# Four chained graph layers on one core: the attended rows written inside the last loop, and edge rows gathered onto a shift

## The reference, cut to what matters

```python
x = _layernorm(x + _L0_gnn_ref(...))        # edge messages, two dense products, norm
x = _layernorm(x + _L1_gnn_ref(...))        # (out - mean) * rsqrt(var) * gamma + beta, leaky relu, + x
x = _layernorm(x + _L2_gnn_ref(...))        # equivariant messages over edges
x = _layernorm(x + _L3_gnn_ref(...))        # attention over edges

# inside layer 3, over the edges that share a src:
aw = jnp.einsum('ehf,ehf->eh', q[src], k[dst])
m = jax.ops.segment_max(aw, src); e = jnp.exp(aw - m[src])
denom = jax.ops.segment_sum(e, src)
out = jax.ops.segment_sum((e / denom[src])[:, :, None] * v[dst], src)
```

## Time and profile before

| | |
|---|---|
| time of 3 runs, median (lowest to highest) | 2148.97 us (2148.57 to 2158.34) |
| the profiled execution | 2156.94 us, its span 2155.2 us |
| busy share of the span | PE 84%, DVE 67%, ACT 53%, POOL 44% |
| mean granted TensorE clock | 0.896 of full speed |
| DMA | 350.61 MB, mean 163 GB/s |

### The profile page before, as it was taken

How to read it: one execution, slowest core, us unless ns; L and a number is a source line. 1 busy time by engine, 2 the same in 40 slices (tenths; PEclk the granted TensorE clock), 3 DMA queues, 4 the chain that set the end, 5 groups by cost and what they waited for, 6 DMA issues and landing times. The chain is left out here.

```text
span 2155.2 us, 24520 instructions
## 1 busy us (share of the span) xinstructions
PE 1803.9 (84%) x5525; PEld 933.2 (43%) x5525; DVE 1434.7 (67%) x2621; ACT 1149.2 (53%) x2356; POOL 949.1 (44%) x1070
## 2 busy tenths in 40 slices
PE   5999999599999999999999995961881588998840
PEld 2444444244444444444444443531771344544420
DVE  5365554177777777777777773517995578787876
ACT  1344434255555555555555552224883878877853
POOL 2212102166666666656666663544553232333236
PEclk8999999799999999999999997985555689999965
DMA  7752102534444454444444445554556887878774
GB/s 250 250 206 63 27 13 31 142 134 172 171 159 166 157 172 172 165 164 155 169 172 172 163 153 188 105 87 156 110 119 178 257 242 221 238 212 241 200 212 144
DMA packets 167421, 350.61 MB, mean 163 GB/s; under 512 B 30481, under 2 KB 30962, under 8 KB 166838
## 3 DMA queue, kind: packets, MB, share of 16 engines
q1 hardware_dynamic: 130838, 247.28, 32.4%
q0 software_dynamic: 33168, 98.01, 20.4%
q10 hardware_dynamic: 3344, 4.51, 0.7%
HBM read 177.32 MB, written 153.71 MB: 154 GB/s over the span
## 5 line engine op out<-in xcount | busy, mean ns | idle before, releaser
L687 PE MATMUL d_p_h<-w3a,d_xT 128*128 128x512 f32 x632 | 285.6, 595 | 23.2 <-DMA d_xT<-in_xT 23.2
L687 PE MATMUL d_p_p<-d_wr,d_x1T 128*128 128x512 f32 x632 | 288.3, 600 | 0.0
L687 PE MATMUL d_p_o<-d_w,d_uT 128*128 128x512 f32 x632 | 284.5, 593 | 3.0 <-ACT d_uT L762 3.0
L562 POOL TENSOR_SCALAR d_small<-d_mv 128x1 f32<-128x1 f32 x158 | 77.6, 491 | 296.7 <-DVE d_mv L813 148.7
L851 DVE TENSOR_TENSOR d_zz<-d_yg,d_xbeta 128x512 f32<-128x512 f32 x79 | 136.9, 1733 | 96.3 <-POOL d_yg L902 96.3
L687 PEld LDWEIGHTS d_p_h<-w3a,d_xT 128*128 128x128 f32 x632 | 120.7, 191 | 175.6 <-issue 175.6
L687 PEld LDWEIGHTS d_p_o<-d_w,d_uT 128*128 128x128 f32 x632 | 119.8, 190 | 153.7 <-issue 149.1
L755 ACT ACTIVATE d_yn<-d_y,d_small 128x512 f32<-128x512 f32 x79 | 64.3, 814 | 228.2 <-POOL d_small L567 228.2
L687 PEld LDWEIGHTS d_p_p<-d_wr,d_x1T 128*128 128x128 f32 x632 | 115.6, 193 | 116.5 <-issue 116.5
L783 ACT ACTIVATE d_x<-d_zz,d_small 128x512 f32<-128x512 f32 x79 | 64.2, 813 | 174.9 <-POOL d_small L567 174.9
L294 PE MATMUL m_p_H<-m_xT,m_w 128*128 128x512 f32 x320 | 146.8, 613 | 4.8 <-ACT m_xT L335 4.8
(11 more groups left out here) (286 smaller groups left out, 4080.9 us busy)
## 6 DMA issues: line engine op xcount, KB each, us to landing
sum_counted<-m_tile_sum SPq DMA_DIRECT2D x10, 2112.0 KB
state<-d_empty SPq DMA_DIRECT2D x80, 264.0 KB, 2.4
update<-d_empty SPq DMA_DIRECT2D x80, 256.0 KB, 2.3
pair_x<-x SPq DMA_DIRECT2D x40, 512.0 KB
out_rows<-pair_rows SPq DMA_DIRECT2D x40, 512.0 KB
d_xT<-in_xT SPq DMA_DIRECT2D x79, 256.0 KB
d_z<-sum_counted SPq DMA_DIRECT2D x79, 256.0 KB
d_x<-in_x SPq DMA_DIRECT2D x79, 256.0 KB
```

The costliest lines, as they stand in the source:

```text
L562: nc.gpsimd.tensor_scalar(tmp, var, factor, add, ALU.mult, ALU.add).then_inc(done, 1)
L687: last = nc.tensor.matmul(out[:, :], lhsT[:, c, :], w[:, c, :], start=(c == 0), stop=(c == KB - 1))
```

## The change

Four edits.

1. The tail goes. In step s DVE runs `attend(s-4)` on the state that it has just merged: reciprocal, product, addition of the src row (in place, in `src_rows_sb`), statistics. ACT runs `source_rows(s-4)`, the normalisation, ahead of the late part of its tiles. The state is not gathered again. Since a state is final only when a src occurs for the last time, the table in stage `a_` now marks the last occurrence in place of the first (19 comparisons, of 23240 columns in all where there were 24320). POOL scatters the 20 tiles of rows at the ends of steps 21, 22 and 23: 8, 9 and 3 of them (`WRITTEN`).
2. `plain_plan` is 2 pairs in each of steps 0 to 19 and none in the last four; ACT takes up to 4 tiles in a step.
3. Four pairs in place of three are loaded plainly (`PLAIN`).
4. In the edge stage the quotient is computed between `norm(0)` and `norm(1)`. From tile 2 on, SP fills the buffer of the src end with the quotient, POOL gathers p onto it by an accumulating indirect DMA, and DVE adds the shift to the dst end alone (128x512).

```diff
-PLAIN = 3
+PLAIN = 4
...
-            for t in range(1, T):
-                ready(nc.vector.tensor_scalar(equal[:, 0:t * P], rows_i[:, 0:t * P], col_f[:, 0, t:t + 1], None,
+            for t in range(T - 1):
+                later = min((t + 1) * P, LAST_START)
+                ready(nc.vector.tensor_scalar(equal[:, later:E], rows_i[:, later:E], col_f[:, 0, t:t + 1], None,
...
-    plan = [3, 3, 2, 2] + [2 - i % 2 for i in range(steps - 6)] + [1, 2]
+    plan = [2] * (steps - 4) + [0] * 4
...
-        n = given - done if step < 5 or step == len(plan) else min(given - done, 3)
+        n = given - done if step < 5 or step == len(plan) else min(given - done, 4)
...
-            pair_fill(nc, k, sp, PLAIN)
+            sp.wait_ge(k.quotient_done, 1)
+            for t in range(2, T):
+                sp.wait_ge(src_scaled, t - 1)
+                sp.dma_start(other[(2 * t + 1) % 4][:, :], k.quotient[:, :]).then_inc(filled[t % 2], 16)
...
+                    t = u // 2
+                    pool.wait_ge(filled[t % 2], 16 * (t // 2))
+                    pool.indirect_dma_start(other[u % 4][:, :], None, k.p[:, :], at_rows(k.index[:, 0, t:t + 1]),
+                                            compute_op=ALU.add).then_inc(added[t % 2], 16)
+                    return
...
-                nc.vector.tensor_tensor(a[b][:, :, :], a[b][:, :, :], wide(k.bn_shift), ALU.add).then_inc(shifted, 1)
+                ends = a[b][:, :, :] if t < 2 else a[b][:, 0:1, :]
+                shift_row = wide(k.bn_shift) if t < 2 else k.bn_shift[:, :].rearrange("p (a d) -> p a d", a=1)
+                nc.vector.tensor_tensor(ends, ends, shift_row, ALU.add).then_inc(shifted, 1)
...
+        WRITTEN = (0, 8, T - 3, T)
...
+                if step == STEPS - 3:
+                    for b in range(ROW_BUFS):
+                        pool.wait_ge(k.pair_gone[b], 16 * (PAIRS // ROW_BUFS))
+                if step >= STEPS - 3:
+                    for i in range(WRITTEN[step - STEPS + 3], WRITTEN[step - STEPS + 4]):
+                        scatter_out(i)
...
+            def source_rows(t):
+                b, row = t % 2, k.src_rows_sb[:, t, :]
+                act.wait_ge(o_ready, t + 1)
+                reciprocal_deviation(nc, k, act, o_mv[b][:, 1:2], o_neg[b], o_rstd[b][:, :], o_shift[b], o_sc, 3 * t)
+                nc.scalar.activation(row, row, ACT.Identity, bias=o_shift[b][:, 0:1], scale=o_rstd[b][:, 0:1]
+                                     ).then_inc(out_done, 1)
...
+                if 0 <= e < T:
+                    attend(e)
                 for j in range(pair + 1, pair + HERE[step]):
                     pair_leaky(nc, k, dve, j)
                     pair_means(nc, k, dve, j)
```

More of the change, by code:

```diff
@@ L1440, in _ @@
                     norm(t)
+                if t == 0:
+                    quotient()
                 if t >= 2:
                     message(t - 2)
[L1444 to L1449, removed]
-                n += 1
-                dve.wait_ge(k.quotient_steps, n)
-            nc.vector.tensor_tensor(k.quotient[:, :], k.bn_shift[:, :], small, ALU.mult).then_inc(k.quotient_done, 1)
         @block.scalar
@@ L1656, in _ @@
             pair_store(nc, k, sp, PAIRS - 1)
-            for b in range(ROWS_AHEAD):
-                sp.wait_ge(out_gone[b], 32 * len(range(b, G, ROWS_AHEAD)))
+            sp.wait_ge(out_gone, 16 * T)
         @block.gpsimd
@@ L1949, in _ @@
                 unit += TILES[step]
-            for g in range(G):
-                b, rows = g % 2, y[g % ROWS_AHEAD]
-                act.wait_ge(o_ready, g + 1)
-                reciprocal_deviation(nc, k, act, o_mv[b][:, :, 1], o_neg[b], o_rstd[b][:, :], o_shift[b], o_sc, 4 * g)
-                for s in range(2):
-                    nc.scalar.activation(rows[:, s, :], rows[:, s, :], ACT.Identity, bias=o_shift[b][:, s:s + 1],
-                                         scale=o_rstd[b][:, s:s + 1]).then_inc(out_done, 1)
         @block.vector
@@ L2048, in merge, with attend @@
                 nc.vector.tensor_tensor(state_parts(new), state_parts(new), part[:, :, :], ALU.add).then_inc(merged, 1)
+            def attend(t):
+                b, row, mean = t % 2, k.src_rows_sb[:, t, :], part[:, :, 0:HD]
+                dve.wait_ge(merged, t + 1)
+                if t:
+                    dve.wait_ge(att, t)
+                nc.vector.reciprocal(inv[:, :], state_parts(new)[:, :, HD]).then_inc(inv_done, 1)
+                dve.wait_ge(inv_done, t + 1)
+                if t:
+                    dve.wait_ge(o_y_done, t)
+                nc.vector.tensor_tensor(mean, state_parts(new)[:, :, 0:HD],
+                                        inv[:, :].rearrange("p (h a) -> p h a", a=1).to_broadcast([P, HEADS, HD]),
+                                        ALU.mult).then_inc(att, 1)
+                dve.wait_ge(att, t + 1)
+                nc.vector.tensor_tensor(row.rearrange("p (h f) -> p h f", h=HEADS), mean,
+                                        row.rearrange("p (h f) -> p h f", h=HEADS), ALU.add).then_inc(o_y_done, 1)
+                dve.wait_ge(o_y_done, t + 1)
+                if t >= 2:
+                    dve.wait_ge(out_done, t - 1)
+                nc.vector.bn_stats(o_stats[b][:, :], row).then_inc(st, 1)
+                dve.wait_ge(st, t + 1)
+                nc.vector.bn_aggr(o_mv[b][:, :], o_stats[b][:, :]).then_inc(mv_done, 1)
+                dve.wait_ge(mv_done, t + 1)
+                nc.vector.tensor_scalar(o_neg[b][:, :], o_mv[b][:, 0:1], -1.0, None, ALU.mult).then_inc(o_ready, 1)
             pair = 0
```

110 lines of the change are left out of this document (34 added, 76 removed).

## The result

| | time, us (lowest to highest) | against the kernel before |
|---|---|---|
| before, beside it on the same chip (20 runs) | 2154.44 (2148.57 to 2162.53) | |
| changed kernel (20 runs) | 2165.63 (2151.00 to 2175.23) | 1.0046, interval 1.0032 to 1.0060 |

The changed kernel is slower by 0.46%, about 10 us, where I had forecast a gain of 0.9 us. The time lies inside the range; the sign and the likeliest case were wrong. Of the 17.6 us between 2148 and the median, 5.5 are the kernel before itself, which ran at 2154.44 here and not at 2148.97. The profiled execution took 2168.74 us with a span of 2167.0, 11.8 over the span of before. One execution among all that follow, 2351.42 us at a granted clock of 0.79, fell in a slower state of the chip and is left out of its version's ratio.

A forecast was written before the change was run, and what follows sets the result against it. Pair-buffer reuse was taken to bound the last stage at 22.9 us a step; its span gain of 7.4 us and the edge stage's loss of 6.5 gave -0.9, so 2148 us, range 2118 to 2174.

The forecast's parts named there:

- Two pairs in a step, the ring: Last stage, steps with two pairs: pair-buffer reuse sets the step at 22.9 us, over DVE's 21.
- the ring: Pair-buffer loop in the last stage: late tile's store, fill, p addition, POOL's scatter and gathers; 45.6 us for two steps.
- DVE's own sum: DVE's work in a two-pair step: 19.9 us, with waiting for ACT a bound of 21.
- rival B: PE's clock falls in part of each last-stage step, delaying values and attended rows: 20 us slower, 2168; chance 0.20.
- edge stage: Edge stage with moved quotient and accumulating gathers: 6.0 + 3.2 - 2.7, so 6.5 us lost.
- step 20: Last stage, step without a pair on DVE but four tiles on ACT: 20.7 us, from ACT's 15.8.
- merge 17 to the last scatter's end: POOL's closing list of state scatters, state gathers and output scatters: 42.9 us, with 6.5 from state scatter to gather.
- the walk to pair 10: Last stage up to pair 10, now first of step 5: starts at 1736, 3 us later than before.
- edge stage's closed chain: Edge stage, norm over ACT's list, scatter, gather and landing to a later norm: 5.8 or 6.2 us a period, 6.0 taken.
- Rival A: Last stage: DVE binds, not buffer reuse; 21.0 us a step, 27 us less, 2121; chance 0.34 with cases between.
- rule of the Trainium skill: GpSimd DMA costs 2.0 us plus bytes over 436 GB/s: 3.2 us per pair-buffer transfer, some 8 us less over two steps.
- Rival C: Edge stage's accumulating gathers take 6.8 us a period: 14 us more, 2162; chance 0.10.

The follow-up runs named there:

- the best order: Changed kernel with the old edge stage, source rows behind the late tile, and one early tile instead of two: 2139.82 us, 0.9920 of the kernel before.

## Why the prediction was wrong

**The step that failed.** It is the part "Two pairs in a step, the ring": the 22.9 us, and with the next part the claim that the ring lies over everything else in a step. The ring did not bind. It was also too long by 0.5 or more: in the version with one early tile and a busy PE, which keeps the late tile behind the source rows as the changed kernel does, DVE waits for p rows and the step is 22.4. (The 22.05 of the best order belongs to a shorter ring, in which the late tile waits neither for attend nor for the source rows.) The period of 23.9 comes from K1, for which the prediction had most of the pieces (attend 2.5, source rows 1.7, late tile 2.4, the early tile ahead of the query copy) but put them into the ring alone or into DVE's own sum. The low clock of queries and values, 4.7 us of K1, it weighed only as rival B. It never walked from ScalarE's late tile over the queries, the scores and the values back to the attended rows. In the loop of the kernel before ACT had no source rows, and so nothing there waited for attended rows on DVE; the change adds this wait, and the prediction named what it delays (the late tile's store) but not the copies and queries queued behind it.

**The account.** Against the forecast span of 2154.3, the measured 2167.0 is 12.7 over:

| term | forecast | measured | difference |
|---|---|---|---|
| edge stage | +6.5 | +5.5 | -1.0 |
| start of pair 10, edge included | 1742.5 | 1743.8 | +1.3, so +2.3 beside the edge stage |
| pair 10 to pair 38 | 320.6 | 331.7 | +11.1 |
| to the merge of tile 16 | 19.9 | 23.3 | +3.4 |
| step 20 | 20.7 | 22.8 | +2.1 |
| merge 17 to the last scatter's end | 42.9 | 39.6 | -3.3 |
| to the end of the span | 7.7 | 5.9 | -1.8 |

The merge of tile 16 is the same error once more: it ends a step of K1. At the end the state's scatter and gather follow each other by 3.0 us (2122.51 to 2125.52) and 3.5, where I had taken 6.5 from a row in the middle of the loop. There the DMA engines are busy 0.78 of the time, at the end 0.34.

**Right.** The tail is gone, the walk to pair 10 holds to 2.3 us, the edge stage costs what was forecast, by the steps forecast: quotient 5.9 for 6.0, tile 2's wait 2.7 for 3.2, and 3.1 back for 2.7. The clean effect on the median, some 8 us in the edge edits' own run, is above the 5.5 of this trace. Two terms were sound in result and loose in working. The edge stage's closed chain adds up to 5.7 and 6.1 us a period by the prediction's own terms, where it says 5.8 and 6.2; measured are 6.01. And ACT's 15.8 us a step, in the term of step 20, stands in no row: by the earlier trace rows ACT is busy 270.9 / 18.7 = 14.5.

**The rivals.** Rival B had the price (2168) and the clock (0.8 granted, 0.80 measured), with values that come late and delay the attended rows. DVE does wait for them, 1.19 us in each step, and their low clock is 1.7 us of K1. Where it put this delay, into the ring, it was wrong; the clock counts through queries and values in K1. That its price of 2168 lies 2 us from the median is partly luck: 5.5 us of that are the kernel before. Rival A was right that the ring does not bind and wrong in its price of 21.0, since DVE is not the bound either. The rule of the Trainium skill weighed there (DMA: Bandwidth & Descriptors, Anatomy of one DMA) spoke for such a slack: by it the ring is some 4 us a step shorter than by my rows. Measured, it is some 0.5 shorter, so the rows were nearer. The rule is also one for transfers that GpSimd issues, and the ring's store and fill are issued by SP. Rival C did not come: the edge tiles follow at 6.01 us on average, as forecast, not at 6.8.

## What to carry to other kernels

When a change adds a wait on an in-order engine, follow what is queued behind the waiting instruction all the way until the walk comes back to the producer, and add up the circle; compare it with every other circle of the loop before calling one the bound. Several circles can lie within 2 us of each other, as three did here (23.9, 23.1 to 25, 22.0 to 22.4), and then an edit that cuts one alone shows nothing or a loss; try edits in pairs before dropping them. An instruction that waits for another engine's last result belongs behind everything on its engine that does not need it, as the source rows did here, though that paid only with the second circle cut.

## What the runs showed of the hardware

After 3.61 us without work PE ran its next eight products of 128x512 at a granted clock of 0.50 and then 0.58, 6.71 us for the eight; with small products in the gap they took 3.70. After 4.80 us idle the 16 small products of the spread took 3.77 in place of 2.05. After 2.49 us idle it was sometimes the one and sometimes the other. The eight products of the values, which follow the spread without a wait, took 5.37 us (0.50 at first) in most steps of the changed kernel, and 3.70 in most of the kernel before. A wait on PE's path is thus paid twice, and filling it with useless products paid only where nothing else held the step (2147 us against 2174). Which of two neighbouring groups of products bears the low clock changed with the place of the wait, so a reordering on ScalarE moved it from the queries to the spread, and the step went from 23.75 to 25.6 us without any change of work.
